# Preparing the first tile, loading the K sums and finishing the last two tiles in another order

## The reference

```python
def attn(x):                       # H=16 heads of DH=64
    q, k, v = heads(x @ Wq), heads(x @ Wk), heads(x @ Wv)
    q, k = elu(q) + 1, elu(k) + 1
    z = einsum('bhnd,bhd->bhn', q, k.sum(axis=2))[..., None] + 1e-6
    out = einsum('bhnd,bhde->bhne', q, einsum('bhnd,bhne->bhde', k, v)) / z
    return merge(out) @ Wo + bo

def ffn(x):                        # y: square of relu, then a projection
    y = square(relu(x @ W_fc.T)) @ W_proj.T
    # 5 steps: mem = 0.9*mem + y - (mem > 1); spike = mem > 1
    return number_of_spikes(y) / 5

x = x + attn(layernorm(x))
x = x + ffn(layernorm(x))
```

## Time and profile before

| what | value |
|---|---|
| median of 3 runs | 1037.02 us (1036.47 to 1037.12) |
| profiled execution: its own time | 1036.43 us |
| profiled execution: span | 1034.6 us |
| PE busy | 1026.2 us (99%), 6999 matmuls |
| DVE busy | 873.8 us (84%) |
| ACT busy | 737.3 us (71%) |
| POOL busy | 654.7 us (63%) |
| mean granted TensorE clock | 1.000 |
| PE waiting for x, once at the start | 2.9 us |
| PE waiting for DMA xT<-xnat later on | 0.4 us, once |

### The profile page before, as it was taken

How to read it: one execution, slowest core, us unless ns; L and a number is a source line. 1 busy time by engine, 2 the same in 40 slices (tenths; PEclk the granted TensorE clock), 3 DMA queues, 4 the chain that set the end, 5 groups by cost and what they waited for, 6 DMA issues and landing times.

```text
span 1034.6 us, 19797 instructions
## 1 busy us (share of the span) xinstructions
PE 1026.2 (99%) x6999; PEld 653.0 (63%) x6999; DVE 873.8 (84%) x1871; ACT 737.3 (71%) x1216; POOL 654.7 (63%) x410
## 2 busy tenths in 40 slices
PE   8999999999999999999999999999999999999998
PEld 4444444444444467777777767777777777777887
DVE  7899887898888699888888888888888888888875
ACT  8888677778768758676666767676767676676664
POOL 1444434455345488777778676878777777777835
PEclk9999999999999999999999999999999999999999
DMA  4546553225323545454454454455444444544441
GB/s 132 148 127 145 121 122 88 77 63 122 87 69 82 122 76 113 93 107 99 96 128 108 82 105 95 105 106 98 97 108 108 93 103 107 108 93 93 78 80 45
DMA packets 265284, 104.24 MB, mean 101 GB/s; under 512 B 219360, under 2 KB 262624, under 8 KB 265184
## 3 DMA queue, kind: packets, MB, share of 16 engines
q1 hardware_dynamic: 265040, 102.90, 44.7%
q10 hardware_dynamic: 144, 0.07, 0.0%
HBM read 33.69 MB, written 16.79 MB: 49 GB/s over the span
## 4 chain that ended last, share of the span: by engine, by line
PE 97%; DMA 1%; DVE 1%; ACT 1%; issue 0%; ACTq 0%; DVEq 0%
PE proj L619 31%; PE acc L784 16%; PE acc L820 16%; PE acc L662 15%; PE acc L759 8%; PE acc L768 4%; PE acc L761 4%; PE proj L696 1%; PE proj L684 1%; DMA xT<-xnat 1%; ACT feat L879 0%; PE acc L633 0%; PE proj L673 0%; DMA x_t<-in_L_attn_x_dram 0%; ACT feat L875 0%
## 5 line engine op out<-in xcount | busy, mean ns | idle before, releaser
L875 ACT ACTIVATE feat<-proj 128x1024 f32<-128x1024 f32 x123 | 125.7, 1022 | 193.7 <-PE proj L619 193.7
L1555 POOL TENSOR_TENSOR qT<-qT,feat 128x1024 f32<-128x1024 f32 x60 | 142.4, 2373 | 174.8 <-DVE xnat L1186 151.3
L1590 POOL TENSOR_TENSOR h<-h_f,h 128x512 f16<-128x512 f32 x128 | 148.8, 1183 | 159.2 <-ACT h L1052 159.2
L784 PE MATMUL acc<-xn2T,wfcT 128*128 128x256 f16 x1536 | 178.0, 273 | 0.0
L820 PE MATMUL acc<-wpT,h 128*128 128x256 f16 (+1 forms) x1560 | 177.9, 271 | 0.1
L662 PE MATMUL acc<-feat,xnat 128*128 128x512 f16 x768 | 176.2, 379 | 0.0
L619 PE MATMUL proj<-wk,xT 128*128 128x512 f16 x756 | 173.3, 379 | 0.7 <-DMA xT<-xnat 0.4
L784 PEld LDWEIGHTS acc<-xn2T,wfcT 128*128 128x128 f16 x1536 | 150.3, 98 | 28.9
L1561 POOL TENSOR_TENSOR feat<-feat,rz 128x1024 f32<-128x1024 f32 x60 | 165.8, 2764 | 2.8 <-DVE rz L1293 2.8
L619 PE MATMUL proj<-wq,xT 128*128 128x512 f16 x720 | 165.2, 379 | 0.0
L820 PEld LDWEIGHTS acc<-wpT,h 128*128 128x128 f16 x1560 | 150.6, 98 | 22.7 <-issue 0.3
(11 more groups left out here) (106 smaller groups left out, 1317.9 us busy)
## 6 DMA issues: line engine op xcount, KB each, us to landing
x_t<-in_L_attn_x_dram SPq DMA_DIRECT2D x128, 128.0 KB, 2.3
xT_spill<-xT SPq DMA_DIRECT2D x64, 128.0 KB, 2.0
out_dram<-out_t SPq DMA_DIRECT2D x63, 128.0 KB, 2.1
xT<-xT_spill SPq DMA_DIRECT2D x60, 128.0 KB, 2.3
ks_all<-ks_rows SPq DMA_DIRECT2D x4, 512.0 KB, 4.5
qT<-feat SPq DMA_TRANSPOSE x120, 3.1
m_all<-in_L_attn_Wk_dram SPq DMA_DIRECT2D x4, 256.0 KB, 4.3
xT<-xnat SPq DMA_TRANSPOSE x64, 2.4
```

Of the source, the lines that this page charges most:

```text
L784: mm = pe.matmul(acc[:, 2 + g % 2, f % 2 * 2 * P:(f % 2 + 1) * 2 * P], wfcT[:, left, f * C2 + c2, :], xn2T[:, pair % 4, right * C2 + c2, : ...
L1555: pool.tensor_tensor(kacc[:, b % 2, :], kacc[:, b % 2, :], k_feat(n), ALU.add).then_inc(k_added, 1)
L1590: pool.tensor_tensor(lo, h_f[:, k % 4, :], hi, ALU.subtract).then_inc(h_lo, 1)
```

## The change

Four things are changed.

- **First turn.** Tile 0 is turned by two DMA transposes: its high half, two blocks, as soon as that is written (semaphore first_turned), and its low half after it. `first_k_tile` takes its 12 matmuls in another order, with the three high-by-high ones that need only the first piece ahead. Six `keep_warm` matmuls before it go, with their waits. `spill_xn(0)` waits for both pieces.
- **Newton.** The iteration of tiles 1 to 3 is done by GpSimd (`newton_early`), ahead of its K sums; VectorE waits for all of it before `first_lo(0)`.
- **K sums.** `load_ks` is issued six rounds after its guest, not five.
- **Last two tiles.** f2 of tile 62 is made in halves as well, in banks 1 and 3, with parts of the two halves in turn (`f2_part`, `f2_halves`); tile 63 uses banks 0 and 2 as before. VectorE takes the steps of both tiles in one order written out by hand (`last_two_spikes`).

```diff
+            sp.wait_ge(ln1.hi, 1)
+            sp.dma_start_transpose(xT[:, 0, 0:C2, :], xnat[:, 0, HI, :]).then_inc(first_turned, 16)
+            sp.wait_ge(ln1.lo, 1)
+            sp.dma_start_transpose(xT[:, 0, C2:2 * C2, :], xnat[:, 0, LO, :]).then_inc(xnT_ready[0], 16)
-            turn_xn(0)
...
-                if n - 5 in GUESTS and GUESTS[n - 5][0] == "kv":
-                    load_ks(GUESTS[n - 5][1])
+                if n - 6 in GUESTS and GUESTS[n - 6][0] == "kv":
+                    load_ks(GUESTS[n - 6][1])
...
+                pe.wait_ge(first_turned, 16)
+                pe.wait_ge(w_hi, 1)
+                part(0, 0, HI, HI)          # half, c2, left, right
+                pe.wait_ge(w_hi, 2)
+                part(0, 1, HI, HI)
+                pe.wait_ge(w_hi, 3)
+                part(1, 0, HI, HI)
+                pe.wait_ge(xnT_ready[0], 16)
+                part(0, 0, LO, HI)
+                part(0, 1, LO, HI)
+                pe.wait_ge(w_split, 1)
+                part(0, 0, HI, LO)
+                pe.wait_ge(w_split, 2)
+                part(0, 1, HI, LO).then_inc(k_half_proj, 1)
+                part(1, 0, LO, HI)
+                pe.wait_ge(w_split, 3)
+                part(1, 0, HI, LO)
+                pe.wait_ge(w_hi, 4)
+                part(1, 1, HI, HI)
+                part(1, 1, LO, HI)
+                pe.wait_ge(w_split, 4)
+                part(1, 1, HI, LO).then_inc(k_proj, 1)
...
             pe.wait_ge(ln1.newton, 6)
             keep_warm(4)
-            pe.wait_ge(ln1.hi, 2)
-            keep_warm(4)
-            pe.wait_ge(ln1.lo, 2)
-            keep_warm(2)
             first_k_tile()
...
+            def f2_halves(n):
+                pair = n // 2
+                pe.wait_ge(h_relu, 4 * pair + 4)
+                pe.wait_ge(spike_steps, 5 * HALVED)
+                for done in half_steps:
+                    pe.wait_ge(done, 5 * (n - 1 - HALVED))
+                if n == PARTED:             # TILES - 2
+                    pe.wait_ge(h_lo, 4 * pair + 2)
+                    f2_part(n, 0, range(0, 6))
+                    f2_part(n, 1, range(0, 3))
+                    f2_part(n, 0, range(6, FB))
+                    f2_part(n, 1, range(3, FB))
+                else:
+                    for half in range(2):
+                        f2_part(n, half, range(FB))
...
-            newton(ln1, 1)
-            newton(ln1, 2)
-            newton(ln1, 3)
+            dve.wait_ge(ln1.newton, 3 * CENTRED)      # before first_lo(0)
...
+            def last_two_spikes():
+                n, last = PARTED, TILES - 1
+                half_step(n, 0, 0)
+                half_step(n, 1, 0)
+                half_step(n, 0, 1)
+                half_step(n, 2, 0)
+                half_step(n, 1, 1)
+                half_step(n, 3, 0)
+                half_step(n, 2, 1)
+                half_step(n, 4, 0)
+                half_step(n, 3, 1)
+                half_step(last, 0, 0)
+                half_step(n, 4, 1)
+                for k in range(1, 5):
+                    half_step(last, k, 0)
+                half_step(last, 0, 1)
+                write_half(0)
+                for k in range(1, 5):
+                    half_step(last, k, 1)
+                write_half(1)
...
+            def newton_early(n):              # on GpSimd, n = 1, 2, 3
+                u = n % 4
+                r0, p, q, r1 = seed[:, u:u + 1], newt[:, u, 0:1], newt[:, u, 1:2], newt[:, u, 2:3]
+                pool.wait_ge(ln1.seed, n + 1)
+                pool.wait_ge(ln1.newton, 3 * n)
+                pool.tensor_scalar(p, mv[:, u, 1:2], LN_EPS, r0, ALU.add, ALU.mult).then_inc(ln1.newton, 1)
+                pool.wait_ge(ln1.newton, 3 * n + 1)
+                pool.tensor_scalar(q, p, r0, 0.5, ALU.mult, ALU.mult).then_inc(ln1.newton, 1)
+                pool.wait_ge(ln1.newton, 3 * n + 2)
+                pool.tensor_scalar(r1, q, -1.5, r0, ALU.add, ALU.mult).then_inc(ln1.newton, 1)
```

More of the change, by code:

```diff
@@ L263, in y_at, with half_y @@
             return acc[:, 1 - (n % 2 if n >= TILES - 6 else 0), 0:D]
-        def last_y(half):
-            return (y_at(TILES - 1) if half == 0 else acc[:, 2, 0:D])[:, 0:P]
+        PARTED = TILES - 2
+        def half_y(n, half):
+            bank = 1 - n % 2 + 2 * half
+            return acc[:, bank, 0:P] if n >= PARTED else y_at(n)[:, half_cols(half)]
         def spikes_at(n):
@@ L624, in first_k_tile, with part @@
             def first_k_tile():
-                pe.wait_ge(xnT_ready[0], 16)
[L627 to L637, removed]
+                def part(half, c2, left, right):
+                    cols = slice(half * HALF, (half + 1) * HALF)
+                    return pe.matmul(k_place(0)[:, cols], xT[:, 0, left * C2 + c2, :], wk[:, right, c2, cols],
+                                     start=(c2 == 0 and left == HI and right == HI),
+                                     stop=(c2 == C2 - 1 and right == LO))
+                pe.wait_ge(first_turned, 16)
[5 more added lines that the diff above has]
+                part(1, 0, HI, HI)
+                pe.wait_ge(xnT_ready[0], 16)
+                part(0, 0, LO, HI)
[12 more added lines that the diff above has]
+                part(1, 1, HI, LO).then_inc(k_proj, 1)
             def q_tile(n):
@@ L795, in f2_tile @@
                 pair, u = n // 2, n % 2
-                last = n == TILES - 2
                 if u == 0:
-                    pe.wait_ge(h_lo, 4 * pair + (2 if last else 4))
+                    pe.wait_ge(h_lo, 4 * pair + 4)
                 if n == 0:
@@ L806, in f2_tile @@
                     wait_past(pe, done, 5 * (before - HALVED))
[L807 to L821, removed]
-                    mm.then_inc(f2_done, 1)
+                i = 0
@@ new lines, in f2_tile, with f2_part @@
+                for f in range(FB):
+                    for left, right in PRODUCTS:
+                        i += 1
+                        mm = pe.matmul(y_at(n), h[:, pair % 2, left, f, u * P:(u + 1) * P], wpT[:, right, f::FB, :],
+                                       start=(i == 1), stop=(i == FB * len(PRODUCTS)))
+                mm.then_inc(f2_done, 1)
+            def f2_part(n, half, blocks):
+                pair, u = n // 2, n % 2
+                for f in blocks:
+                    if u == 0 and half == 0 and f >= FB // 2 and f % 2 == 0:
+                        pe.wait_ge(h_lo, 4 * pair + f // 2 + 1)
+                    for left, right in PRODUCTS:
+                        mm = pe.matmul(half_y(n, half), h[:, pair % 2, left, f, u * P:(u + 1) * P],
+                                       wpT[:, right, half * FB + f, :],
+                                       start=(f == 0 and (left, right) == PRODUCTS[0]),
+                                       stop=(f == FB - 1 and (left, right) == PRODUCTS[-1]))
+                if f == FB - 1:
+                    mm.then_inc(f2_done, 1)
@@ L1571, in q_lo_tile @@
                     done.then_inc(q_lo, 1)
+            def newton_early(n):
[8 more added lines that the diff above has]
+                pool.tensor_scalar(r1, q, -1.5, r0, ALU.add, ALU.mult).then_inc(ln1.newton, 1)
+            for n in range(1, CENTRED):
+                newton_early(n)
             for n in range(TILES):
```

25 lines of the change are left out of this document (12 added, 13 removed).

## The result

| | median us | runs (lowest to highest) | profiled execution | its span |
|---|---|---|---|---|
| before | 1036.51 | 22 (1035.92 to 1037.29) | 1036.43 | 1034.6 |
| after | 1037.87 | 22 (1037.55 to 1039.61) | 1037.71 | 1035.9 |

What follows compares the result with a forecast made beforehand. TensorE, 97% of the span, bounds the kernel, so only its standstills pay. Head -0.50, middle -0.52 and tail +0.26 sum to -0.76: 1035.7 us against 1036.43 (1036.3 against the median); 8-in-10 range 1035.2 to 1037.9.

Steps and rivals of the forecast that it cites:

- Head, (b): Newton on GpSimd: first_neg(0) comes 2.35-6x us earlier, x being one 128x1 step, taken as 0.30; whole head gains 0.50.
- 3.20-9x: Gain in us at k_tile(3), x being one GpSimd Newton step; the head gains the smaller of this and 0.75.
- Rival 1: GpSimd's column step in the head is slower: at 0.40 us, +0.2 (1037.2); at 0.5, +1.0 (1038.1); chance 0.20.
- Rival 5: One-time setup on GpSimd falls on Newton in the head: +3.6 us (1040.7), by the skill +5.2; chance 0.03.
- 9.03+6x: Start in us of first_neg(0) in the head, 11.38 in before, x being one GpSimd Newton step.
- Head, (a): First turn in two pieces: second lands at 8.95, fewer matmuls follow it, k_half_proj at about 10.1 instead of 11.36.
- rival 2: The first turn's second piece lands late, at 9.8: head gain 0.2, sum -0.5 us (1036.6); chance 0.12.
- The warm-up matmuls: Those removed in the head stood in TensorE's idle time; their removal was priced at nothing.
- Middle: load_ks one round later removes TensorE's stall near 341: gain 0.52 us, bounds 0 and 0.6.
- Rival 4: The middle stall only moves: sum -0.24 us (1036.8); chance 0.05.
- Tail: Tile 63's first step waits for GpSimd's addition for tile 61: last write 0.26 us later, bounds 0 and +0.35.
- Rival 3: The tail is free, GpSimd's tile 61 coming out earlier than its row: sum -1.0 us (1036.0); chance 0.10.

Runs made afterwards that it cites:

- Experiment 6: Kernel before with the first turn in two pieces and load_ks one round later, the six warm-up matmuls kept: 1035.54 us, -0.79 against before.
- experiment 5: Kernel before with the first turn in two pieces, load_ks one round later and six warm-up matmuls fewer: 1036.86 us, +0.53 against before.
- experiment 11: Kernel before with only the Newton of tiles 1 to 3 moved to GpSimd: 1036.94 us, +0.65 against before.
- experiment 4: Kernel before with only load_ks one round later: 1036.07 us, -0.29 against before.
- experiments 3: Kernel after with the six warm-up matmuls put back: 1037.65 us, +1.29 against before.

## Why the prediction was wrong

**Head, (b): the step that failed.** I asked for one number, "the time of one 128x1 Newton step", and bounded it by the instruction alone. The value was near: 0.30 taken (the rule given there makes 0.31), 0.26 or 0.27 measured where nothing holds GpSimd. What the two long steps took was not a property of the step but of what VectorE runs beside it, and my own order of work put split_lo there: in before Newton stood on VectorE's queue, so it couldn't overlap it. 9x was in fact 0.86 (tile 1) plus 1.85 (tile 2) plus 0.80 (tile 3), 3.51 in place of 2.70, and nearly all the excess, 0.98 more than 3 x 0.29, fell on the tile that first_neg(0) waits for. The line "3.20-9x" with that sum gives -0.31 where -0.51 was measured at k_tile(3). Of the other 0.20, 0.11 is not the kernel's: in this execution the first x tile came later (tile 1's seed at 6.35 for 6.24). The rest lies in handovers of a few hundredths each. Rival 1 named the right place and sign (GpSimd's column step) and the wrong reason, an x of 0.4 or more for all steps alike. Rival 5 is out: the first TENSOR_SCALAR on GpSimd took 0.33 and started 0.11 behind the seed, so setup cost nothing. The Trainium skill (GPSIMD Engine Reference, Instruction dispatch) gives about 6 us for the first call of a freshly loaded kernel; this trace can't tell, because GpSimd is idle for 6.23 us ahead of that step. The factor of about 2 that the prediction took from the Trainium skill (GPSIMD Engine Reference, Engine selection) is stated there for two-input operations, and the same row calls one-input ones roughly line-rate; a Newton step has one tensor input. Measured is 0.27 against VectorE's 0.21, 1.3.

The prediction's own numbers also said that this part had nothing to win. With the turn in pieces and Newton left on VectorE, tile 2's high half stands at 10.41 and first_neg(0) can follow 0.41 later, at 10.82; by 9.03+6x it stands at 10.83 for x=0.30. Experiment 6 measured 10.88 with Newton on VectorE, and had the head's gain. It was the two edits together that were priced at 0.50, and never each alone.

**Head, (a).** Two pieces hold SP 1.28 and 1.23 (1.3 taken). The second landed at 9.39, between the 8.95 taken and rival 2's 9.8: 2.42, what a later turn of four blocks takes, so the landing did not shrink with the blocks. The first piece took 3.27 and landed at 8.90. That the pieces bring about 0.5 in the head is right (k_tile(4) at 24.51 for 25.06 in experiment 6).

**The warm-up matmuls.** "Stood in TensorE's idle time" is true, and their time was nothing; their place in the program was not nothing. This is the second step that failed, a term put at nothing: 0.62 at k_tile(6), which experiments 5 and 6 tie to the six matmuls and experiment 11 to Newton's move. I had priced every moved DMA that the kernel issues, and none of those that the chip issues for its engines. The page's third part named them, in lines I did not read (q8 and q14, kind "instruction").

**Middle.** Right: 0.52 predicted, 0.58 with the small stall at 154, and alone in experiment 4. Rival 4 is out.

**Tail.** The wait was right: VectorE waits for the addition of tile 61. The size was off, 0.83 for 0.26. Tile 63's first step came 4.65 after tile 62's first matmul, for 4.52 worked out: the addition ended 0.04 late, and its handover took 0.13 for 0.04. Half 1's first step added 0.03. The rest, 0.40, is write_half(0) at 0.68 for 0.28, and all behind it moves. It is the mechanism of the head again. Rival 3 is out.

**Sum.** The forecast -0.76; replace the head's term (+0.98), add the fetches (+0.62), the middle's (-0.06) and the tail's (+0.57): +1.35. By experiments from the kernel before, the parts alone are -0.29 (K sums), +0.65 (Newton), +1.02 (tail) and, turn with K sums less K sums, +0.82: together 2.2, more than the 1.36 of all. They needn't add up: the turn (experiment 5) and Newton (experiment 11) each have a stall at 31 when alone, and together there is one. The medians' intervals are wide enough to hold part of the gap as well.

**Range.** 1037.87 lies just inside the 8-in-10 range, which ended at 1037.9. That is luck: the range was set from 1037.02, the median of 3 runs, and the 22 runs of before have 1036.51. A loss of 1.36 is beyond the 0.9 that the range allowed.

## What to carry to other kernels

Before moving work from VectorE to GpSimd, list what VectorE will run beside it: an instruction with two SBUF inputs there makes a 0.27 us step take 0.8, and a GpSimd addition makes a 0.28 us write take 0.68; put VectorE's PSUM-fed instructions beside GpSimd's work, or order the two apart. In a kernel whose queues are full, taking instructions out of an engine's stream, idle ones too, moves the fetches of code; look where the "instruction" packets fall in both traces before pricing a stall. Bound an unknown duration by what stands beside it, not only by the rows of its kind. Price each part of a change alone before pricing them together.

## What the runs showed of the hardware

- A fetch of 16 KB follows TensorE's place in its program, one of 8 KB VectorE's: the first moved from 20.5 to 24.4 us with six matmuls less, the second stayed (experiments 6 and 5); with VectorE's Newton gone the second moved from 21.7 to 27.8 and the first stayed within 0.7 (experiment 11).
- Where TensorE's fetch fell into loads in flight, the x load landed in 4.4 to 4.8 us in place of 2.3, and one weight load held SP for 1.9 to 2.5 us in six of seven traces. Where only VectorE's was late (experiments 3 and 11), the x load kept its 2.2 to 2.4 and the turn behind it landed in 3.9 to 4.1 in place of 2.8 to 3.0. How a fetch does that the traces don't show.
- Turns of two blocks take SP 1.23 to 1.29. The second piece lands in 2.4 to 2.6 us, the first in 3.1 to 3.6. Turns of four blocks take 1.19 and land in 2.4 when little else is in flight; the first one of the kernel before, and of those that turn it whole, took 1.30 and landed in 2.7 to 3.3.
- A GpSimd operation on one column takes 0.26 or 0.27 us, and the next starts a tenth of a microsecond after it. Beside a VectorE operation with two inputs in SBUF it ended 0.13 to 0.14 us behind that one's end, however long that took (0.33, 0.76, 0.82).
